# Layer statistics by bn_stats and bn_aggr in two of three normalisations of an audio tower, with a new order of steps

## The reference

```python
def _layernorm(x, eps=1e-05):
    m = mean(x, -1); v = var(x, -1)
    return (x - m) / sqrt(v + eps)
# token part: four dense layers of 64x64, then a strided convolution
out = X
for i in range(2): out = tanh(out @ W_in[i] + b_in[i])
out = abs(core_diag) * out * out
for i in range(2): out = tanh(out @ W_out[1 - i] + b_out[1 - i])
h = conv(pad(out, 7), filter of 15 taps, stride 2, the same for each channel)
# attention without softmax
xn = _layernorm(h)
logits = relu(where(causal, (xn Wq.T) (xn Wk.T).T, 0)) / max(row, 1)
h = h + logits (xn Wv.T) Wo.T
# 16 experts of 64 -> 128 -> 64, two of them weighted for each token
x = _layernorm(h)
top-2 of x @ gate_w + gate_b, softmax over the two
moe = weighted sum of relu(x @ w1[e] + b1[e]) @ w2[e] + b2[e]
y = x + moe
h = h + (y - mean(y)) / sqrt(var(y) + eps) * gamma + beta
```

## Time and profile before

| | us |
|---|---|
| median of 3 runs | 193.9 |
| lowest, highest | 193.89, 196.59 |
| profiled execution | 194.28 |
| its span | 192.1 |

### The profile page before, as it was taken

One profiled execution on the slowest core, in us unless ns is written; L12 is line 12 of the kernel. 1 busy time (PEld: TensorE's weight loads), 2 busy tenths in 40 slices (PEclk: granted clock), 3 DMA queues, 4 the chain that ended last, 5 costly groups with the idle time before them and its releaser, 6 DMA issues.

```text
span 192.1 us, 3827 instructions
## 1 busy us (share of the span) xinstructions
PE 162.3 (85%) x1474; PEld 92.4 (48%) x1474; DVE 112.5 (59%) x283; ACT 90.3 (47%) x158; POOL 37.7 (20%) x52
## 2 busy tenths in 40 slices
PE   0789599998852989999998999999999988999810
PEld 0455367685731845443455353453754435455410
DVE  0644556638697268867249987467698345572141
ACT  0223356546323137655545636547365662666410
POOL 6553001154331102400002510003032001120030
...
GB/s 157 58 76 206 99 73 136 134 75 2 3 0 0 68 203 243 148 0 3 52 198 235 181 45 7 101 195 246 118 0 13 105 241 247 102 45 0 0 3 40
...
## 3 DMA queue, kind: packets, MB, share of 16 engines
...
q10 hardware_dynamic: 713, 0.32, 0.6%
...
## 4 chain that ended last, share of the span: by engine, by line
PE 43%; SPq 14%; DMA 13%; issue 13%; POOL 7%; DVE 5%; ACT 1%; POOLq 1%; DVEq 0%; ACTq 0%
PE y L947 14%; PE z L934 14%; DMA w_last<-in_L_ffn_w_dram 6%; SPq L369 5%; SPq L365 3%; PE a L867 3%; SPq L336 3%; DMA out_dram<-y_out 3%; POOL w_s L526 3%; PE z L835 2%; PE a L876 2%; DMA gate_all<-gates_dram 2%; DMA filt_row<-n_L_tok_conv_filter_dram 2%; PE z L913 2%; PE a L897 2%
## 5 line engine op out<-in xcount | busy, mean ns | idle before, releaser
L468 ACT ACTIVATE hid<-z 128x750 f32<-128x750 f32 x64 | 50.7, 796 | 36.7 <-PE z L934 36.3
L947 PE MATMUL y<-hid,w_s 64*64 64x375 f32 x512 | 59.1, 483 | 0.3 <-ACT hid L468 0.3
L934 PE MATMUL z<-xg,w_s 64*64 64x375 f32 x512 | 58.8, 477 | 0.0
L771 DVE TENSOR_TENSOR xg<-xa_t,gate_all 128x375 f32<-128x375 f32 x64 | 35.8, 584 | 19.8 <-PE z L934 11.0
L934 PEld LDWEIGHTS z<-xg,w_s 64*64 64x64 f32 x512 | 22.5, 132 | 19.1 <-issue 15.5
L947 PEld LDWEIGHTS y<-hid,w_s 64*64 64x64 f32 x512 | 19.9, 131 | 19.5 <-ACT hid L468 9.4
L530 POOL TENSOR_TENSOR stat_A<-stat_A,minus_half 125x6 f32<-125x6 f32 x4 | 5.8, 1460 | 51.6 <-DVE stat_A L592 51.5
L530 POOL TENSOR_TENSOR stat_F<-stat_F,minus_half 125x6 f32<-125x6 f32 x4 | 6.0, 1503 | 41.4 <-DVE stat_F L592 41.4
L695 DVE SCALAR_TENSOR_TENSOR attn<-a,causal_cap 125x125 f32<-125x125 f32 (+1 forms) x16 | 5.3, 351 | 13.0 <-PE a L867 12.5
L530 POOL TENSOR_TENSOR stat_T<-stat_T,minus_half 125x6 f32<-125x6 f32 x4 | 5.7, 1431 | 36.4 <-DVE stat_T L592 36.4
L637 DVE COPY x_in<-x_raw 125x384 f32<-125x384 f32 x8 | 4.0, 546 | 10.6 <-DMA x_raw<-in_x_dram 10.6
...
## 6 DMA issues: line engine op xcount, KB each, us to landing
...
gate_all<-gates_dram SPq DMA_DIRECT2D x16, 93.8 KB, 2.8
...
out_dram<-y_out SPq DMA_DIRECT2D x8, 93.8 KB
...
```

The lines of the kernel that those rows point to most:

```text
L468: act.activation(hid[:, n % HID], z_pair[e % 2][:, :, 0:TO], ACT.Relu).then_inc(hid_ready.sem, 1)
L771: nc.vector.tensor_tensor(xg[:, n % XG], xa_t[g % 2][:], gate_all[:, e], ALU.mult).then_inc(xg_ready.sem, 1)
L934: ins = mm(z[e % 2][b][q, 0:TO], w1_s[f, e, q], xg[f, n % XG], start=True, stop=True)
L947: ins = mm(y[h][b * D:(b + 1) * D, 0:TO], w2_s[q, e, :], hid[q, (E * g + e) % HID, b], start=e == 0, stop=e == E - 1)
```

## The change

The normalisations "T" and "A" get mean and variance from two instructions of VectorE, `bn_stats` (for each of the six groups of 64 values, the statistics of its two halves) and `bn_aggr` (which puts them together). `square` and `variance` are gone from both, and with them the steps T6 and A5 on ScalarE and T7 and A6 on VectorE. The centring now comes last in `center`, after the signal on which POOL's power waits. `normalise` waits for the centring too. The third normalisation "F" is as before.

```diff
             def center(k, g, src):
-                link, st = chains[k].at(g), stat[k]
-                link(nc.vector.tensor_reduce(st[:, 0, :], src[:], AX.X, ALU.add))
-                nc.vector.scalar_tensor_tensor(out=cent[k][:], in0=wide(st[:, 0, :]), scalar=1.0 / D, in1=src[:],
-                                               op0=ALU.mult, op1=ALU.subtract, reverse1=True)\
-                    .then_inc(ln_cent[k].sem, 1)
+                link = chains[k].at(g)
+                for j in range(NJ):
+                    ins = nc.vector.bn_stats(out=halves_of[k][:, j, :], in_=src[:, j, :])
+                link(ins)
+                for j in range(NJ):
+                    ins = nc.vector.bn_aggr(out=mean_var[k][:, j, :], in_=halves_of[k][:, j, :])
+                link(ins)
+                nc.vector.tensor_scalar(stat[k][:, 1, :], mean_var[k][:, :, 1], EPS, None, ALU.add).then_inc(ln_var[k].sem, 1)
+                nc.vector.tensor_tensor(cent[k][:], src[:], wide(mean_var[k][:, :, 0]), ALU.subtract).then_inc(ln_cent[k].sem, 1)
...
             def normalise(k, g, dst):
+                dve.wait_ge(ln_cent[k].sem, ln_cent[k].after(g, 1))
                 dve.wait_ge(ln_rstd[k].sem, ln_rstd[k].after(g, 1))
...
                     act.copy(hres[g][:].rearrange("p j d -> p (j d)"),
                              banks[0][0:TOK, 0:NJ * D]).then_inc(hres_ready.sem, 1)
-                elif s == 6:
-                    square("T", g)
...
-                elif s == 5:
-                    square("A", g)
...
-                elif s == 7:
-                    variance("T", g)
...
-                elif s == 6:
-                    variance("A", g)
                 elif s == 7:
                     if g == 0:
                         dve.wait_ge(const_pool, 6)
+                    dve.wait_ge(ln_cent["A"].sem, ln_cent["A"].after(g, 1))
                     dve.wait_ge(ln_rstd["A"].sem, ln_rstd["A"].after(g, 1))
...
-                T0.7 S0.10 S0.11 S0.12 S0.13 A0.6 T1.7 F0.0 T2.7 T3.7 A1.6 A2.6 F0.3 F1.0 A3.6 F1.3 F2.0 F2.3 F3.0
+                T0.7 S0.10 S0.11 S0.12 S0.13 T1.7 A0.6 F0.0 T2.7 T3.7 A1.6 A2.6 F0.3 F1.0 A3.6 F1.3 F2.0 F2.3 F3.0
...
-                A0.12 A1.12 F0.5 A2.12 A3.12 F1.5 F2.5 F3.5""",
+                A0.12 A1.12 F0.5 A2.12 F1.5 A3.12 F2.5 F3.5""",
```

More of the change, by code:

```diff
@@ L144, in audio_tower @@
         cent = {k: sb(f"cent_{k}", [TOK, NJ, D]) for k in "TAF"}
-        csq = {k: sb(f"csq_{k}", [TOK, NJ, D]) for k in "TAF"}
+        csq = {"F": sb("csq_F", [TOK, NJ, D])}
+        halves_of = {k: sb(f"halves_{k}", [TOK, NJ, 6]) for k in "TA"}
+        mean_var = {k: sb(f"mean_var_{k}", [TOK, NJ, 2]) for k in "TA"}
         stat = {k: sb(f"stat_{k}", [TOK, 3, NJ]) for k in "TAF"}
@@ L204, in audio_tower @@
         ln_cent = {k: signal(f"ln_cent_{k}") for k in "TAF"}
-        ln_sq = {k: signal(f"ln_sq_{k}") for k in "TAF"}
+        ln_sq = {"F": signal("ln_sq_F")}
         ln_var = {k: signal(f"ln_var_{k}") for k in "TAF"}
@@ L258, in audio_tower @@
[L258 to L262, removed]
+                in0.12 A1.12 out0.11 in0.13 A2.2 out0.12 in0.14 A2.3 out0.13 in0.15 A2.4 out0.14 out0.15 A2.5 in1.0
@@ L267, in audio_tower @@
[L267 to L271, removed]
@@ new lines, in audio_tower @@
+                S0.0 T0.1 T0.2 T0.3 T1.1 T0.4 T1.2 T2.1 T1.3 T0.5 T2.2 A0.0 T1.4 A0.1 T2.3 A0.2 T3.1 T1.5 A0.3 T3.2
+                A0.4 T3.3 A0.8 T2.4 A1.0 A0.10 A1.1 T2.5 A0.12 T3.4 A1.2 A1.3 T3.5 A1.4 in0.0 in0.1 in0.2 in0.3
+                in0.4 in0.5 in0.6 A1.8 in0.7 A2.0 in0.8 A2.1 in0.9 A1.10 in0.10 in0.11 in0.12 A1.12 in0.13 A2.2
+                in0.14 A2.3 in0.15 A2.4 F0.0 in1.0 in1.1 F0.2 in1.2 in1.3 in1.4 A2.8 in1.5 A3.0 A3.1 in1.6 in1.7
+                A2.10 in1.8 in1.9 in1.10 A2.12 in1.11 A3.2 in1.12 A3.3 in1.13 A3.4 in1.14 in1.15 in2.0 F1.0 in2.1
@@ new lines, in audio_tower @@
+                F1.2 A3.8 in2.2 in2.3 in2.4 in2.5 in2.6 in2.7 A3.10 in2.8 in2.9 A3.12 in2.10 in2.11 in2.12 in2.13
+                in2.14 in2.15 in3.0 F2.0 in3.1 F2.2 in3.2 in3.3 in3.4 in3.5 in3.6 in3.7 in3.8 in3.9 in3.10 in3.11
+                in3.12 in3.13 in3.14 in3.15 F3.0 F3.2""",
+            "vector": """
+                X0.0 T0.0 X1.0 T1.0 S0.8 S0.1 X2.0 T0.2 X3.0 S0.2 T0.4 T2.0 T1.2 S0.5 T0.6 T1.4 T0.8 T2.2 T3.0 S0.6
+                A0.2 A0.3 T1.6 T3.2 T2.4 A0.5 T1.8 A0.7 T3.4 A0.9 A0.10 A0.11 T2.6 A1.2 A1.3 T2.8 gate0.0 gate0.1
+                gate0.2 gate0.3 T3.6 gate0.4 A1.5 gate0.5 gate0.6 A1.7 gate0.7 gate0.8 gate0.9 gate0.10 A1.9
+                gate0.11 A1.10 gate0.12 A1.11 gate0.13 T3.8 gate0.14 gate0.15 A2.2 A2.3 gate1.0 gate1.1 F0.0
+                gate1.2 A2.5 F0.2 gate1.3 F0.3 gate1.4 A2.7 gate1.5 F0.4 gate1.6 gate1.7 A2.9 gate1.8 A2.10 gate1.9
+                gate1.10 A2.11 gate1.11 gate1.12 gate1.13 gate1.14 gate1.15 A3.2 A3.3 gate2.0 gate2.1 gate2.2 A3.5
+                gate2.3 F1.0 gate2.4 gate2.5 A3.7 F1.2 F1.3 gate2.6 gate2.7 A3.9 F1.4 gate2.8 A3.10 gate2.9 A3.11
+                gate2.10 gate2.11 gate2.12 gate2.13 gate2.14 gate2.15 gate3.0 gate3.1 gate3.2 gate3.3 gate3.4 F2.0
+                gate3.5 F2.2 F2.3 gate3.6 gate3.7 F2.4 gate3.8 gate3.9 gate3.10 gate3.11 gate3.12 gate3.13 gate3.14
+                gate3.15 F3.0 F3.2 F3.3 F3.4""",
```

29 lines of the change are left out of this document (10 added, 19 removed).

## The result

| | before | changed |
|---|---|---|
| median, us | 194.55 | 203.55 |
| lowest, highest | 193.89, 196.59 | 201.50, 204.34 |
| profiled execution, its span | 194.28, 192.1 | 201.50, 199.3 |

The ratio is 1.044, 95% interval 1.0367 to 1.0514: slower by 9 us, outside the predicted range of 189.2 to 195.8. Four executions each stand behind the medians (with the fourth, of 195.19, the median of the kernel before is 194.55 and no longer 193.9); 201.5 is the shortest of the changed kernel's four, so its profile shows the least of the loss, 7.2 us.

A forecast was written before the change was run, and what follows sets the result against it. The prediction took the moment of in0.0, plus expert work, its waits and a tail, as the bound. From 194.28, -2.8 -0.8 +2.2 = -1.4 gave 192.9, 192.5 by the median, stated as 192.4; range 189.2 to 195.8.

The forecast's parts named there:

- The price of the statistics: Each changed normalisation, first bn_stats to POOL's power: 1.7 us instead of 2.68, a gain of 1.0.
- Step (1): Front, pair 0's convolution: T2.1 at 25.4, convolution ends 0.9 later, yet xn1 of pair 0 about 0.4 earlier.
- Step (3): Front, second normalisation: it gives 1.0 us, so xa stays at 52.4.
- Step (4): Front, VectorE: T2.6 no longer between A0.9 and A0.10, saving 1.06 us; A0.12 at 59.85 instead of 60.90.
- Step (5)/(6): Front, T2.5 moved before A1.1: in0.0 gains 4.2 us at full clock, 2.8 if it falls before T2.5 (taken).
- Turns of the pairs: Waits before F0.1 (0.76 us, goes) and at F1.1 (some 0.3): a gain of 0.8 us for both.
- The replay: Pair 3's gates traced with VectorE's rows: done at 146.0 instead of 143.4, A3.12 at 147.1 instead of 144.84.
- The last gates: Before F2.1: A3.12 is late, the chain through gate_all is fixed, F2.1 at 161.3, a loss of 2.2 us.
- The rivals: Last gates not late (0.25), clock full alone (0.08), clock long at half (0.12), slow bn instructions (0.10); nothing changes, within forecast.
- The one on the slower side: T0 and A0: bn instructions cost 0.29 each without overlap, 4 us lost, total 196.5; chance 0.10.
- The sum itself: Whole kernel: moment of in0.0, unchanged expert work, waits within it and a tail; -2.8 -0.8 +2.2 = -1.4, 192.9.

The follow-up runs named there:

- e9: Changed kernel with one VectorE copy, F2.0 (y_t of pair 2), moved earlier, from behind gate3.4 to behind gate3.1: 198.2 us, ratio 1.0201.
- e17: Changed kernel with y_t of pair 2 early and POOL's F0.0 (h_beta) moved behind T2.7's power: ratio 1.0113 against the kernel before.
- e11: New statistics in the old order of steps, with six VectorE steps moved out of the way: ratio 0.996 against the kernel before.
- e12: New statistics, old order, six VectorE steps moved, plus extra idle matmuls, three before T2.1 and two before A0.12: 193.9 us, ratio 0.9975.
- e14: Kernel before (old statistics, old order) with y_t of pair 2 early and three extra matmuls before T2.1 and three before A0.12: 193.8 us, ratio 0.9923.
- new front: New statistics with the changed order of steps up to A0.12 and the old order behind it: ratio 1.016 against the kernel before.
- new rest: New statistics with the old order of steps up to A0.12 and the changed order behind it: ratio 1.0257 against the kernel before.
- the fills: Changed kernel with extra matmuls outside the computation, three before T2.1 and three before A0.8, where TensorE stood idle: ratio 1.0279 against the kernel before.

## Why the prediction was wrong, step by step

The steps that failed are two terms of the sum: in0.0, forecast 2.8 us earlier and measured 1.2 later, and the stretch behind it, forecast 1.4 longer and measured 6.0 longer. Together these are the 8.6 us between 192.9 and 201.5. Both left out what the new lists put in front of what: the holes with their falls of the clock, and VectorE's blocks.

- **The price of the statistics was right**: 1.7 forecast, 1.76 measured. The Trainium skill ("VectorE: DVE Perf Modes", "The DRAIN you can't avoid") would have had each instruction wait for the one ahead to drain, except where it isn't held. Six bn_stats of 211 ns on average take 0.86 and not 1.27, so the trace shows the exception, not the rule. (By that rule's 2.5 us the prediction's sum comes to 194.1, not 194.5.) What the prediction left out is that nothing gets in between: "VectorE's own work doesn't grow much" is true of the sum (113.5 against 112.5 us) and says nothing of who stands behind it.
- **Step (1)**, the first to fail, foresaw T2.1 at 25.4 (25.26) and put the hole ahead of it at nothing for the clock. The clock fell there; the convolution of pair 0 came 2.5 later, not 0.9. The fall is 1.7 of it: from T2.1 to that convolution it is 4.32 here and 2.63 in `e9`, where the clock stayed full. The rest of the chain carried it: A0.5 at 49.34 against 47.4 forecast, `xa` at 54.49 against 52.4. Whether the clock falls there is in part luck, and even without it `e9` has in0.0 at 71.20, 2.9 behind the forecast.
- **Step (3)** kept `xa` at 0.55; it took 1.26 beside POOL's `h_beta` (`e17`).
- **Step (4)** was right as far as it went: with nothing between A0.9 and A0.10 `e11` has A0.12 at 58.85. **Step (5)/(6)**: the clock fell before T2.5 as thought likelier than not, 4.47 against 4.5. A0.12 stood at 63.87, 2.6 after the forecast, all of it inherited: `xa` was done 2.8 late. Another 1.4 came behind A0.12. `gates_t` stood behind `q_t` and `hres` in ScalarE's list, so the logits waited 1.08 and not 0.44. And T2.6 stands ahead of A1.2 in VectorE's list, so its block held up the causal logits (`attn`), and A1.3 waited 1.56 where 0.8 was forecast. No run moved either; both are read from the rows.

```profile
64.96 0.86 DVE L582 BATCH_NORM_STATS2 halves_T<-hres 125x6 f32<-125x64 f32 x6 [1.75 <-ACT hres L419]
...
66.94 0.47 DVE L696 SCALAR_TENSOR_TENSOR attn<-a,causal_cap 125x125 f32<-125x125 f32 x2
```

- **Turns of the pairs**: -0.8 forecast. The wait before F0.1 shrank by 0.4, the one before F1.1 grew by 0.9 (`y_t` behind A3.5's block), and a new one of 1.14 at 81.0 came from A1.5's block between gate products: +1.6. The replay followed `y_t` and not the blocks.
- **The last gates**: the wait of 3 us before F2.1 came true (2.60 against 1.11 before), for the reason given. But the chain "gates, gate_all, fifth product" was taken as fixed when it was only a place in a list (`e9`), and the fall of the clock behind such a wait (1.6 us here) was priced at the front and nowhere else. From in0.0 to the end 1.4 was forecast, 6.0 measured: 1.6 at the turns, 1.5 at the last gates, 1.6 for the clock, 0.9 of busy time and 0.4 of small waits, which nothing here explains.
- **The rivals**: none had the order as the loss. The one on the slower side priced the instructions, which were the part that held.
- **The sum itself**, "in0.0, plus the expert work, plus the waits", assumed that a gain at in0.0 arrives at the end. `e12` and `e14` are ahead by 4.8 and 2.9 at in0.0 and by 0.9 and 1.8 in the profiled time. Even with a right in0.0 the forecast would have been too low.

Still open: whether new front and new rest lose more together than each alone (2 us by the ratios) and whether the fills and the early copy add up. Neither gap is clear of the noise. Falls of the clock that come and go between executions could make both; that isn't shown.
